# Stacked shares, late values and an unrolled loop in the last head attention of a four-layer gated kernel

## What is computed

```python
x = x + jnp.tanh(g_xattn[3]) * _L3_xattn_ref(_layernorm(x), ctx_4096, mask, L3_xattn_Wq, L3_xattn_Wk, L3_xattn_Wv,
                                             L3_xattn_Wo, L3_xattn_q_norm_w, L3_xattn_k_norm_w)
x = x + jnp.tanh(g_ffn[3]) * _L3_ffn_ref(_layernorm(x), ...)
```

```python
q = _rmsnorm(q, q_norm_w)          # (b, 32, 64, 128)
k = _rmsnorm(jnp.repeat(k, 4, axis=1), k_norm_w)
v = jnp.repeat(v, 4, axis=1)
scores = jnp.einsum('bhqd,bhkd->bhqk', q, k) * scale + mask
probs = softmax(scores)
out = jnp.einsum('bhqk,bhkd->bhqd', probs, v)      # then out @ Wo.T
```

## Time and profile before

| | us |
|---|---|
| median of 3 runs (lowest, highest) | 3316.93 (3313.36, 3325.38) |
| the profiled execution, its own time | 3323.23 |
| its span, first to last instruction | 3321.4 |
| PE busy | 3180.1 (96%) |
| DVE busy | 1708.0 (51%) |
| ACT busy | 1476.6 (44%) |
| POOL busy | 1126.5 (34%) |
| mean granted TensorE clock | 0.990 |

### The profile page before, as it was taken

How to read it: one execution, slowest core, us unless ns; L and a number is a source line. 1 busy time by engine, 2 the same in 40 slices (tenths; PEclk the granted TensorE clock), 3 DMA queues, 4 the chain that set the end, 5 groups by cost and what they waited for, 6 DMA issues and landing times. The chain is left out here.

```text
span 3321.4 us, 55551 instructions
## 1 busy us (share of the span) xinstructions
PE 3180.1 (96%) x21708; PEld 2528.0 (76%) x21708; DVE 1708.0 (51%) x3700; ACT 1476.6 (44%) x3294; POOL 1126.5 (34%) x689
## 2 busy tenths in 40 slices
PE   8998999999999999999999979999999999999997
PEld 5666568888888888888754447888788878888885
DVE  5887543334333433333443666555655655556554
ACT  5776234444444444444322444444444444444443
POOL 6775322232332233222120113333333333344322
PEclk9999999999999999999999989999999999999999
DMA  3000121121122112211012012222111212222201
GB/s 107 2 2 5 40 92 61 64 83 58 64 64 75 66 58 65 64 64 64 14 60 111 13 40 83 69 70 82 64 64 65 82 58 70 70 64 70 73 30 58
DMA packets 56566, 199.93 MB, mean 60 GB/s; under 512 B 8976, under 2 KB 9744, under 8 KB 53008
## 3 DMA queue, kind: packets, MB, share of 16 engines
q1 hardware_dynamic: 56336, 196.76, 17.6%
HBM read 192.54 MB, written 4.19 MB: 59 GB/s over the span
## 5 line engine op out<-in xcount | busy, mean ns | idle before, releaser
L1757 POOL TENSOR_TENSOR h_wol<-h_ro,h_woh 128x1024 fp32r<-128x1024 f32 x128 | 314.4, 2456 | 611.1 <-ACT h_woh L1808 611.1
L1753 POOL TENSOR_TENSOR h_wql<-h_rq,h_wqh 128x1024 fp32r<-128x1024 f32 x128 | 309.0, 2414 | 501.9 <-ACT h_wqh L1803 501.9
L2254 DVE COPY h_tf<-ps 128x512 f32<-128x512 f32 (+1 forms) x256 | 142.6, 557 | 607.2 <-PE ps L2035 607.1
L2258 DVE TENSOR_TENSOR h_ol<-ps,h_oh 128x512 fp32r<-128x512 f32 x256 | 176.8, 691 | 524.1 <-ACT h_oh L1861 524.1
L141 PE MATMUL ps<-h_woh,h_oh 128*128 128x512 f32 x1024 | 427.8, 418 | 5.9 <-DVE h_ol L2258 5.8
L141 PE MATMUL ps<-h_Xh,h_wqh 128*128 128x512 f32 x1024 | 415.1, 405 | 4.1 <-ACT h_sq L1847 1.9
L143 PE MATMUL ps<-h_woh,h_ol 128*128 128x512 f32 x1024 | 405.6, 396 | 0.0
L142 PE MATMUL ps<-h_wol,h_oh 128*128 128x512 f32 x1024 | 404.8, 395 | 0.0
L143 PE MATMUL ps<-h_Xh,h_wql 128*128 128x512 f32 x1024 | 401.7, 392 | 0.0
L142 PE MATMUL ps<-h_Xl,h_wqh 128*128 128x512 f32 x1024 | 400.4, 391 | 0.0
L1911 ACT ACTIVATE h_ex<-ps,h_mx 128x128 f32<-128x128 f32 x512 | 181.3, 366 | 270.8 <-DVE h_mx L2294 270.7
(11 more groups left out here) (298 smaller groups left out, 6316.5 us busy)
## 6 DMA issues: line engine op xcount, KB each, us to landing
h_rq<-in_L_Wq SPq DMA_DIRECT2D x128, 512.0 KB, 3.4
h_ro<-in_L_Wo SPq DMA_DIRECT2D x128, 512.0 KB, 3.4
h_rk<-in_L_Wkv SPq DMA_DIRECT2D x47, 512.0 KB, 3.4
h_craw<-in_ctxT SPq DMA_DIRECT2D x7, 1024.0 KB, 5.7
cnat<-in_ctx SPq DMA_DIRECT2D x4, 1024.0 KB, 8.9
t_craw<-in_ctxT SPq DMA_DIRECT2D x4, 1024.0 KB, 8.7
t_cn<-in_ctx SPq DMA_DIRECT2D x4, 1024.0 KB, 5.3
out_rows<-x SPq DMA_DIRECT2D x16, 256.0 KB, 2.5
```

What stands on the lines that cost most here:

```text
L1753: nc.gpsimd.tensor_tensor(wql[:, par], rq[:, par], f(wqh[:, par]), ALU.subtract).then_inc(m["p_wq"], 1)
L1757: nc.gpsimd.tensor_tensor(wol[:, par], ro[:, par], f(woh[:, par]), ALU.subtract).then_inc(m["p_wo"], 1)
L2254: nc.vector.tensor_copy(tf[:], ps[:, TBK, 0:PT]).then_inc(m["v_t"], 1)
L2258: nc.vector.tensor_tensor(by_head(ol), ps[:, AB, :].rearrange("p (b h t) -> p b h t", h=2, t=S), f(by_head(oh)), ALU.subtract).then_inc(m[ ...
```

## The change

The layer 3 attention gets a function of its own, `phase_heads_last`, a copy of `phase_heads` with `norm=True` in which

- the turned shares of both query pairs are kept, split in a high part in 64 partitions and the rest in the other 64, so that one operand holds both stacked (`tp`); DVE makes both parts, four instructions of 64 partitions in place of one copy;
- the values are split too (`vh`, `vl`); `vh` holds the high part twice, its second copy made by ACT (`values_high`); `values_of` takes four query heads at once, 2 sequences in a call, four fp32r matmuls of 256 columns, and runs four steps behind (`values_of(n - 4)`), the output six (`output(n - 6)`);
- on PE `output` comes ahead of `turn_shares`;
- the values go to DVE in step t = 0 (`values_in`), and `keys_sum` and `keys_norm` stand ahead of `shares_out`;
- Wo's cast and low part come in t = 1 and 2 instead of t = 1 and 3, and Wq and Wo have one load buffer each;
- all heads are written out, with no loop; `add_output` moves to head 1 of the next group, t = 0 and 2.

In `phase_text_ternary` the end of the last group is reordered and the quantiser shortened.

```diff
@@ gelus, end of the ACT list
-                            nc.scalar.preload_act_table_set(LN_EXP)
+                            if g != G - 2:
+                                nc.scalar.preload_act_table_set(LN_EXP)
...
+                        ternary_rows(G - 1)
                         gelus(G - 2)
-                        ternary_rows(G - 1)
@@ quantize
-                            dve.wait_ge(q_xn, NT * g + NT)
-                            own(nc.vector.tensor_reduce(qs[:, 2], rn[:], AX_X, ALU.max, apply_absolute_value=True))
+                            for i in tiles(g):
+                                dve.wait_ge(q_xn, i + 1)
+                                last = nc.vector.tensor_reduce(qs[:, 2, i % NT:i % NT + 1], rn[:, i % NT], AX_X, ALU.max,
+                                                               apply_absolute_value=True)
+                            own(last)
...
-                                last = nc.vector.tensor_scalar(rn[:, j], rn[:, j], qs[:, 3, j:j + 1], -128.0, ALU.mult, ALU.max)
+                                last = nc.vector.tensor_scalar(rn[:, j], rn[:, j], qs[:, 3, j:j + 1], MAGIC, ALU.mult, ALU.add)
...
-                            own(nc.vector.tensor_scalar(rn[:], rn[:], MAGIC, None, ALU.add))
@@ end of the DVE list
+                            if g + 1 == G:
+                                ternary_stats(g)
                             if g:
                                 linear_out(g - 1)
-                        ternary_stats(G - 1)
-                        ternary_add(G - 2)
                         ternary_scale(G - 1)
                         quantize(G - 1)
+                        ternary_add(G - 2)
@@ phase_heads_last: weights and ACT
+                    if t in (1, 2) and it:
+                        k = 2 * (it - 1) + t - 1
+                        o(k, k % NP)
...
+                        def values_high(it):
+                            wait(act, m["s_av"], NS * it)
+                            for b in range(2):
+                                nc.scalar.copy(vh[64 - 64 * b:128 - 64 * b, b::2, :],
+                                               krv[64 * b:64 * b + 64, it % 2, :, 1]).then_inc(m["a_vh"], 1)
...
+                                nc.scalar.activation(ex[:], sc[:], ACT.Exp).then_inc(m["a_e"], 1)
+                                if t == 0 and it:
+                                    values_high(it - 1)
+                                if t in (1, 2) and not end:
+                                    rows_kv(it + 1, t - 1)
+                                if not (end and t >= NS - 2):
+                                    head_out(n + 2, (t + 2) % 4)
+                                if t == NS - 1 and not end:
+                                    keys_turned(it + 1, n + 1)
+                                split_steps(g, i, t, kv, q, o)
+                                if t == 2 and not end:
+                                    keys_root(it + 1)
@@ PE
+                            for b in range(2):
+                                b4 = 2 * (U % 2) + b
+                                for z in (vh, vl):
+                                    last = nc.tensor.matmul(ps[:, AB, 2 * P * b:2 * P * (b + 1)], z[:, HB * half + b4],
+                                                            tp[:, (2 * it + half) % 3, b4].rearrange("p z q -> p (z q)"),
+                                                            start=z is vh, stop=z is vl)
...
+                                if t in (1, 2) and not end:
+                                    wait(pe, m["v_t"], n - 1)
...
+                                    kv_rows(t - 1)
...
+                                if t == NS - 1 and not end:
+                                    wait(pe, m["v_t"], n - 1)
+                                    turn_keys(it + 1)
+                                if n >= 6:
+                                    output(n - 6)
...
+                                if t == NS - 1 and not end:
+                                    pe.wait_ge(m["a_k"], it + 2)
+                                if not start:
+                                    pe.wait_ge(m["v_p"], n)
...
+                                    turn_shares()
+                                if not (end and t == NS - 1):
+                                    if not (end and t == NS - 2):
+                                        pe.wait_ge(m["a_q"], n + 3)
...
+                                    turn_queries(t + 1)
+                                if n >= 4:
+                                    values_of(n - 4)
+                                if g + 1 < G and (i, t) in TURN:
+                                    wait(pe, m["v_t"], n)
+                                    turn_rows(g + 1, TURN[i, t], TBK)
@@ DVE
+                            for b in range(2):
+                                r = slice(64 * b, 64 * b + 64)
+                                nc.vector.tensor_copy(shares_at(n)[r, b::2, :], turned_shares(r)).then_inc(m["v_th"], 1)
+                            for b in range(2):
+                                r = slice(64 * b, 64 * b + 64)
+                                dve.wait_ge(m["v_th"], 2 * n - 1 + b)
+                                last = nc.vector.tensor_tensor(shares_at(n)[64 - 64 * b:128 - 64 * b, b::2, :], turned_shares(r),
+                                                               f(shares_at(n)[r, b::2, :]), ALU.subtract)
...
+                                largest(n, t, own)
+                                if t == 0 and it:
+                                    values_in(it - 1)
+                                if t == 2 and not end:
+                                    keys_sum(it + 1)
+                                    keys_norm(it + 1)
+                                if not start:
+                                    shares_out(n)
+                                shares(n, own, start)
+                                if n >= 4:
+                                    out_low(n - 4)
+                                if not (end and t == NS - 1):
+                                    queries_sum(n + 1)
@@ the call
-        heads3 = phase_heads("3", 8, 2, S, True, a["L3_Wq"], a["L3_Wo"], a["L3_Wkv"], 3)
+        heads3 = phase_heads_last("3", 8, S, a["L3_Wq"], a["L3_Wo"], a["L3_Wkv"], 3)
```

535 lines of the change are left out of this document (added).

## The result

The changed kernel takes 3427.6 us (3424.4 to 3429.7), the kernel before 3316.7: a ratio of 1.033 with a 95% interval of 1.031 to 1.035. The profiled execution has a span of 3423.8 us (before 3321.4) at a mean granted TensorE clock of 0.985. It is 102.4 us longer, and the starts of the turned keys (one `turn_keys` a head) divide that: the first comes 6.7 us earlier (1990.49 against 1997.21), the second 2.2 closer behind it (27.91 against 30.08), the 30 intervals that follow take 1271.8 us instead of 1188.6 (+83.2), and from the last turned keys to the next stage it is 74.3 us instead of 46.1 (+28.2).

The account below looks back on a forecast made before the run. PE was taken to bound the kernel before, single waits to decide after. Heads +63, group turns +12, clock +5, ends +8, phase before -6 gave +82 on 3323.2: 3405, less 6.3 to the median, 3399 us (3275 to 3440).

Parts of the forecast that it names:

- theory (D): The forecast itself: in the last head attention single waits between engines cost more than PE gains; 3399 us, chance 0.62.
- Quiet head: A head of the last head attention without a group turn: 40.3 us against 38.18, +63 over 30 heads.
- the walk: Chain of single waits between DVE, ACT, POOL and PE, followed through a head's four steps: stalls of 4.5 us a head.
- keys' copy: PE waits for the copy of the turned keys before turning the shares in t=3: stall 2.0 us a head.
- query copy: PE waits for the copy of the queries before turning them in t=0: stall 1.5 us a head.
- values product: On PE, four matmuls of 256 columns at 0.124 each: 0.50 us instead of 0.98, saving 0.48 to 0.50 a step.
- Group turns and clock: Three preparations of the next rows, +4 us each, +12 (0 to 30); lowered clock behind longer pauses, +5 (0 to 40).
- Ends: Start and end of the last head attention: late outputs and values take 19 us instead of some 10; +8 (0 to 12).
- The phase before: Phase ahead of the last head attention: additions 3, reduction 1.7 and a pass 1.2 leave the path; -6 us (-3 to -8).
- (A): Rival: in the last head attention the chain does not bind and PE's gain arrives; 3246 us, half the stalls 3285; chance 0.20.
- (B): Rival: PE's gain and the stalls cancel in the last head attention, head 38.1 us, total 3320; chance 0.10.
- (C): Rival: pauses of 1.5 to 2.0 us, two a head, often lower the clock; once a head +50, 3450 us; chance 0.08.

Follow-up runs that it names:

- x_tail: Changed kernel with the last pairs' Wo loaded and split in the idle Wq buffers within the last head: 3421.6 us against 3427.6.
- x_text: Kernel before with only the edits of the phase ahead of the last head attention: 3316.2 us, ratio 0.999.
- x_short: Changed kernel with several edits at once, among them share and values high copies on ACT, Wo ahead of Wq on POOL, DVE work reordered: 3304.7 us, ratio 0.996.
- x_kv: Changed kernel with ACT's cast of the key-value weights in t=3 moved behind the output's high part: 3421.0 us, ratio 1.032.
- x_root: Changed kernel with the keys' root on ACT ahead of the casts of Wq and Wo in t=2: 3429.8 us, ratio 1.034.
- x_vh: Changed kernel with ACT's two values copies moved from t=0 to t=3, behind the output's high part: 3425.5 us, ratio 1.033.
- x_nolow: Changed kernel with the low part of the turned shares left out after the first 12 steps, two share instructions instead of four: 3408.8 us, ratio 1.026.

## Why the prediction was right, and where it was not

The forecast was 3399 (3275 to 3440) with theory (D), the waits of the chain costing more than PE gains; 3427.6 lies in the range, 29 above the point. Of these 29, 8 are no term of the sum: the forecast takes off the 6.3 by which the profiled execution of before lay above the median, and that of the changed kernel lay 2.0 below its own. On the profiled executions the sum said +82 and it was +102.4: quiet heads 12.6 more than said (30 x 2.52 = 75.6 for 63), group turns and clock 9.4 less, the ends 18 more, the phase before 0.7 less. The mechanism was right; that the sum came this near is in part luck, since these errors have both signs.

*Quiet head.* Forecast 40.3, measured 40.70. The waits have the places and almost the lengths of the walk: 1.87 for 2.0 (keys' copy), 1.63 for 1.5 (query copy), and the share instructions 1.80 for 1.77. The Trainium skill (VectorE: DVE Perf Modes, Two Vector instructions with no wait between them) holds such an instruction back until all earlier ones are done, and the trace agrees: 0.45 from start to start, where the one copy of before had 0.34 for all 128 partitions. (The two subtractions also wait for the copies by semaphore, so the pair of copies alone bears on that rule.) In bulk DVE got 7.06 us a head more (28.36 for 21.30), as counted. The key product waits once, 0.32, not twice 0.5: in t=1 the wait for the query copy ahead of it has covered it. PE's own work is 36.8, not 35.9: the values product gained 0.32 a step (0.98 to 0.66) and not 0.48, since the price per product was the mean of a run of 24, in which the dearer first start is spread over many; in a run of four the first has 0.21 and the last 0.22. That step, the values at four times the mean price, was mis-sized by 0.64 us a head; the rest of the 0.9 by which PE's work was taken too low was not traced. The smaller key-product wait gave 0.7 back.

*Group turns and clock.* Forecast 12 + 5; the intervals exceed 30 quiet heads by 50.8 us and did by 43.2 before: +7.6. The wait of the earlier trace rows grew from 2.66 to 3.75 us (forecast 3.9). The lower clock level took 17 spells of 3.4 us in these intervals where it took 4; how much of the +7.6 is theirs was not separated.

*Ends.* Forecast +8, measured +28.2 behind the last turned keys and 2.2 less at the start, +26: this is the step that failed, and most of the miss. It counted the late outputs and values behind the last turned shares as PE work in a row, 19 us for some 10. They took 30.5 (3330.91 to 3361.38) for 9.8 (3249.15 to 3258.94). In them PE waits for the low part of the values product (0.28, 1.40, 1.40; before 0.88 and 1.40) and 4.17 for the last Wo behind its single raw buffer (shown by x_tail, 6 us), and two spells at the lower clock fall in it. Another +7.5 lies between the last turned keys and the last turned shares, for which the sum had no term: the waits of a quiet head (1.88, 1.36), then 2.63 for the low part, 0.51 for Wo and 3.61 for the last multiply.

*The phase before.* Forecast -6, measured -6.7 in the changed kernel at its first turned keys, in one trace of each. The changed kernel and the eleven built on it have no edit between them ahead of that point, and it comes at 1987.2 to 1995.4 in their traces, so the nearness can be chance. By its medians x_text gives 3.5 us (1.7 to 7.3).

*The rivals.* (A) had said that the chain would not bind; PE idle for 3.9 us a head speaks against it, but x_short shows that it is a matter of order: with the same products on PE, and low parts and splits just as many, the head takes 36.76. (B) is out. (C), pauses that lower the clock once a head: not in the quiet heads of the changed kernel (1.00), though in many heads of x_kv and x_root (0.96), in x_kv behind a pause of the same length; and there the slow stretch lay where PE would have waited: in x_root quiet heads at 0.96 take 41.03 us and those at the full clock 41.01 to 41.10.

*What the walk had right for an incomplete reason.* It listed, for each wait of PE, the one arrival that was last. Ahead of the turned queries of t=0 DVE's value instructions ended at 2591.03 where the query copy ended at 2591.01 (x_vh). In t=2 the edit of x_root brought the next arrival itself: with the casts behind the root POOL's second subtraction ends at 2616.96 instead of 2616.38, and it now holds the multiply to 2617.25, where it had ended at 2616.91. For the length of the unchanged walk this made no difference; for what a repair is worth it made all the difference.

## What to carry to other kernels

When work leaves the bounding engine, walk the chain with every arrival at each wait, not the last one alone; a repair is worth the distance to the second, and less where the edit moves the second back. Where one engine's long instruction holds another's, look for the places in the step where it lies beside none of those that it holds, and check that SP's order still lets the raw buffers be filled in time. Price what a longer lag costs at the end as a chain of its own, with its waits, not as a row of products.

## What the runs showed of the hardware

A DVE instruction with two SBUF operands that starts while a POOL `tensor_tensor` runs ends a fixed time behind POOL's end, whenever it starts: with 128x256 elements 0.28 us in the changed kernel (2594.83 against 2594.55), 0.28 in x_nolow (2553.76 against 2553.48) and 0.29 in x_root (2617.25 against 2616.96), with 128x512 elements 0.54. In the last head attention of the changed kernel all 62 multiplies that start beside a subtraction end 0.28 to 0.31 behind it, all 32 normalisations 0.55. The share instructions, which read PSUM, kept their 0.86 and 0.88 beside it. The Trainium skill (GPSIMD Engine Reference, Specifications) lists the contention of POOL with DVE instructions that have two SBUF inputs; these runs agree, and they show its form, a wait until the end and not a slower rate. It goes both ways: a POOL subtraction that starts while such a DVE instruction is under way takes longer, 2.86 us instead of 2.39 beside the normalisation of the changed kernel (from 2613.52 on; DVE until 2614.11), 2.51 beside the low part of the values in x_vh; and that DVE instruction keeps to its own end.

A pause of PE of 1.9 us is followed by the lower clock level for 3.4 us in one kernel (x_kv, granted clock of the head 0.96) and not in another with the same pause (the changed kernel, 1.00). What else decides it was not found here.
